# The radial matmuls of a graph network's second layer on two row groups of TensorE, with the bias as three bf16 parts put in first

## The chip, the cores and the metric

The kernel runs on one core of a Trainium2 chip, in one launch. The metric is the device time of that launch in microseconds. A smaller time is better.

## What is computed

The reference runs four graph layers over 12,500 nodes with 32 features each and 400,000 edges, sorted by destination. Each layer is followed by a sum with its own input and a layer norm. The change touches the second layer only. For it the reference is, cut to what matters:

```python
R = relu(abs_distances[:, None] @ w1 + b1) @ w2 + b2      # w1: 1x64, w2: 64xR_DIM (8x8 values for each path)
Y = spherical_harmonics(rel_vec)                          # Y[0], Y[1:4], Y[4:9] of each edge
Fj = features[src]                                        # 8 scalars and 8 vectors of 3
for i, (mo, lo) in enumerate(RS):                         # RS = [(8, 0), (8, 1)]
    for j, (mi, li) in enumerate(RS):
        Rb = R[:, r_off:r_off + sz].reshape(E, mo, mi, n_lf)
        for k, lf in enumerate(range(abs(lo - li), lo + li + 1)):
            acc = acc + _NORM[i] * einsum('euv,ef,evi,ofi->euo', Rb[..., k], Yf, Fb, C)
msg = concatenate(msg_blocks)                             # 32 values for each edge
out = zeros.at[dst].add(msg)
```

Each edge's distance goes through 64 hidden units into a row R of radial weights. In the kernel 384 of them (after scaling and sorting of the columns) multiply the edge's source features turned into its own frame. b2 is the bias of that row.

## The kernel before

The second layer goes over the edges in 196 groups of 2,048 edges: 128 partitions by T = 16 tiles, in four streams (ST = 4). One group is one `step`, and four groups make one turn of each engine's loop. The order of the work is written out by hand for each engine, and semaphores join them.

- **GpSimd (POOL), L1990 to L2005.** `gathers` issues 16 indirect DMAs for a group, one for each tile, that fetch the source rows into `xg`. There are two `xg` buffers. It waits for one to be free (`fxg`, L1996) and halfway for `half` (L2000), which TensorE raises when it comes to `radial` number 3.
- **SyncE (SP).** `load` brings the distances of a group into `wrow` (64 partitions, all 2,048 edges in each, so that each hidden unit has them), the source indices `s_i` and the nine frame numbers of each edge `e9`. `load_row` brings the flags for the segment sums.
- **ScalarE (ACT).** `hidden` makes `H` = relu(w1 x distance + b1) in partitions 0 to 63, for 2,048 edges in one instruction. Partitions 64 to 127 of `H` hold ones. `spread` copies the turned features into `FG` and `FX` with five copies and frees `xg`. `early_sums` copies the sums of the first four tiles out of PSUM. `scalars` and `scan_store` follow.
- **TensorE (PE).** For each group there are eight calls of `radial(n, u)`. Each makes the rows R of two tiles of 128 edges, tiles 2u and 2u+1, into the two banks of `pR[u % 2]`: one matmul over all 128 rows for each tile, f32, 384 columns. Row 64 of `w2` is the bias and rows 65 to 127 are zeros, so the ones in `H` add the bias. Between the calls stand the early sums (sixteen matmuls on the identity for tiles of u = 0 and 1), `turn` (three matmuls), `columns` and `back` (transposes). The order is radial 0, 1, back, radial 2, 3, early sums (first half), radial 4, early sums (second half), columns, radial 5, turn 0, radial 6, turn 1 and 2, radial 7.
- **VectorE (DVE).** `products(k, u)` waits for `pR` (L2066) and multiplies the two tiles' R with the features: for u = 0 and 1 in three instructions into `PP` (L2069, L2072), for the others in two into `Pr` (L2078, L2080). `sums(k, u)` waits for those products, raises `fpR` (the semaphore that lets TensorE write that `pR` again, L2259 in `radial`) and reduces over the 16 columns (L2089). `head` (L2058), three parts of `tail` and the segment `scan` stand in between.

The matmuls are recorded twice each for f32, since an f32 matmul is two passes over the array; the trace counts each pass. So one `radial` is four matmul records and four weight loads, and 196 groups by 8 by 4 give its 6,272 records.

## Time and profile before

| what | value |
|---|---|
| median of 3 runs | 18,546.1 us |
| lowest and highest run | 18,534.44 and 18,557.52 us |
| span of the profiled execution | 20,972.7 us |
| second layer's loop in that span | from about 6,660 to 12,480 us |

The profiled execution has no time of its own beside its span, and the span is longer than the median of the runs. All rows come from the profiled execution. A row of a timeline gives the start, the duration, the engine, the line, the operation, out<-in with the tile names, how many instructions were merged, and in brackets the idle time of that engine just before, with what ended it. A q behind the engine's name is its sequencer. PEclk is the share of TensorE's full clock that was granted: 1.00 is 2.4 GHz and 0.50 is 1.2 GHz.

### The profile page before, as it was taken

How to read it: one execution, taken by the hardware profiler on the slowest of the kernel's cores; microseconds unless marked ns; L12 is line 12 of the kernel's file. 1: busy time of each engine (PE TensorE's matmuls, PEld its weight loads, DVE VectorE, ACT ScalarE, POOL GpSimd, SP SyncE). 2: the span in 40 equal slices, each digit the busy share in tenths (PEclk: the TensorE clock that was granted, in tenths of full speed). 3: DMA queues.
4: the chain of work that ended last, by engine and by line, in shares of the span. 5: the costliest groups of instructions: out<-in, count | busy, mean ns of one | idle time of the engine just before them, and what ended most of it. 6: DMA issues, size and time to landing. Idle time of an engine off the chain costs nothing. (4 is left out here: it accounts for less than half of the span.)

```text
span 20972.7 us, 293199 instructions
## 1 busy us (share of the span) xinstructions
PE 13068.2 (62%) x92471; PEld 7362.5 (35%) x92471; DVE 11202.5 (53%) x19689; ACT 3071.4 (15%) x5120; POOL 11778.5 (56%) x10055
## 2 busy tenths in 40 slices
PE   0565555555554676776766652555555555699999
PEld 0344434333333444444444431122222112355554
DVE  2565544444444777777777773333332222567777
ACT  0222222222221111111111110111111111000000
POOL 4788888888886555555555554666666665100000
PEclk6565555555556888888888885666666666799999
DMA  7333333333333222222222213333333343489998
GB/s 276 47 39 37 37 39 39 39 37 37 38 39 46 47 49 47 48 47 47 48 46 48 46 40 35 73 70 72 76 71 71 71 76 63 125 257 293 292 293 267
DMA packets 2998639, 1817.14 MB, mean 87 GB/s; under 512 B 1730466, under 2 KB 2755819, under 8 KB 2979019
## 3 DMA queue, kind: packets, MB, share of 16 engines
q1 hardware_dynamic: 2201756, 1336.87, 25.1%
q0 software_dynamic: 669312, 166.80, 11.3%
q10 hardware_dynamic: 126512, 300.38, 4.1%
q8 instruction: 539, 8.83, 0.2%
q14 instruction: 520, 4.25, 0.1%
HBM read 1474.43 MB, written 392.90 MB: 89 GB/s over the span
## 5 line engine op out<-in xcount | busy, mean ns | idle before, releaser
L2005 POOL DMA_INDIRECT xg<-d_tab,s_i x3136 | 3254.6, 1038 | 2615.5 <-POOLq L1996 1630.7
L2537 POOL DMA_INDIRECT xg<-d_tab,s_i x3136 | 2996.6, 956 | 1865.8 <-issue 954.8
L2265 PE MATMUL pR<-w,H 128*128 128x384 f32 x6272 | 2703.4, 560 | 1407.6 <-PEq L2259 834.5
L1403 POOL DMA_INDIRECT d_acc<-AG,ix x1568 | 2471.5, 1576 | 527.2 <-issue 459.5
L1403 POOL DMA_INDIRECT d_acc<-T,ix x1568 | 2466.3, 1573 | 478.3 <-issue 437.1
L2923 PE MATMUL pacc<-nodes,HB 128*32 128x512 fp8e4 x47040 | 2663.0, 380 | 42.7 <-PEq L2967 42.7
L2574 DVE TENSOR_TENSOR_SCAN U<-mU,U,up 128x512 f32<-128x512 f32 x392 | 501.6, 1280 | 3289.0 <-DVEq L2573 2688.6
L2265 PEld LDWEIGHTS pR<-w,H 128*128 128x128 f32 x6272 | 1225.8, 215 | 2533.1 <-issue 2182.8
L2695 PE MATMUL hb<-U,Wbc 128*128 128x512 f32 x784 | 642.4, 914 | 2204.7 <-PEq L2691 2023.1
L1756 PE MATMUL pm<-ms,eq 128*128 128x32 f32 x6272 | 1366.4, 399 | 890.5 <-PEq L1754 888.8
L2923 PEld LDWEIGHTS pacc<-nodes,HB 128*32 128x32 f16 x47040 | 1261.5, 97 | 1317.1 <-issue 57.1
L1756 PEld LDWEIGHTS pm<-ms,eq 128*128 128x128 f32 x6272 | 1344.1, 330 | 934.8 <-issue 934.4
L1035 PE MATMUL pw<-ok,ol 128*128 128x392 bf16 x4048 | 1303.7, 458 | 319.3 <-PEq L1033 299.3
L1023 DVE TENSOR_SCALAR ok<-iotak,kt 128x392 bf16<-128x392 f16 x4048 | 1372.9, 390 | 0.0
L2892 DVE TENSOR_SCALAR nodes<-packed 128x1792 int32<-128x1792 int32 x840 | 918.0, 1093 | 756.3 <-DVEq L2890 755.3
L2078 DVE TENSOR_TENSOR AG<-pR,FG 128x512 f32<-128x512 f32 x784 | 538.0, 686 | 950.3 <-DVEq L2066 893.7
L2695 PEld LDWEIGHTS hb<-U,Wbc 128*128 128x128 f32 x784 | 191.4, 283 | 2313.3 <-issue 2308.3
L2089 DVE TENSOR_REDUCE Q<-AG 128x64 f32<-128x1024 f32 x784 | 948.3, 1210 | 0.0
L2893 DVE TENSOR_SCALAR nodes<-packed 128x1792 int32<-128x1792 int32 x840 | 912.4, 1086 | 0.0
L1718 PE MATMUL sr<-ids,two 2*128 2x512 bf16 x784 | 411.6, 525 | 798.2 <-PEq L1721 794.9
L2271 PE MATMUL pQ<-PP,ident 128*128 128x128 f32 x6272 | 806.4, 281 | 120.4 <-issue 117.9
L2271 PEld LDWEIGHTS pQ<-PP,ident 128*128 128x128 f32 x6272 | 795.8, 197 | 209.0 <-issue 109.7
(338 smaller groups left out, 17504.3 us busy)
## 6 DMA issues: line engine op xcount, KB each, us to landing
packed<-d_A SPq DMA_DIRECT2D x420, 1792.0 KB
row<-d_m SPq DMA_DIRECT2D x1568, 64.0 KB
xg<-d_tab,s_i POOLq DMA_INDIRECT x6272
wrow<-d_w SPq DMA_DIRECT2D x196, 512.0 KB
d_scan<-so ACTq DMA_DIRECT2D x392, 256.0 KB
d_A<-stage ACTq DMA_DIRECT2D x97, 784.0 KB
d_ea<-in_ea_t ACTq DMA_DIRECT2D x1, 50176.0 KB
d_exp<-T ACTq DMA_DIRECT2D x1, 50176.0 KB, 250.4
```

Source lines behind the costliest of these rows:

```text
L1023: last = e.tensor_scalar(ok[:, i, :], A["iotak"][:, :], kt[:, 2, s + i:s + i + 1], kt[:, 1, s + i:s + i + 1], ALU.is_equal, ALU.mult)
L1035: last = e.matmul(A["pw"][w % 2][:, 0:KW], A["ol"][u % RU][:, i, :], A["ok"][u % RU][:, i, :], start=(u % 2 == 0 and i == 0), stop=(u % 2 ...
L1403: e.indirect_dma_start(out=d_acc[i], out_offset=bass.IndirectOffsetOnAxis(ap=ix[k][:, t:t + 1], axis=0), in_=mo[k][:, t * F:(t + 1) * F], ...
L1756: last = e.matmul(pm[:, t, :], eq[k][:, t, :], ms[:, t % CH * ST + t // CH, :], start=True, stop=True)
L2005: e.indirect_dma_start(out=xg[k][:, t, :], out_offset=None, in_=d_tab, in_offset=bass.IndirectOffsetOnAxis(ap=s_i[n][:, t:t + 1], axis=0)) ...
L2089: e.tensor_reduce(Q[k][:, :, 2 * u:2 * u + 2, :].rearrange("p r t u -> p t r u"), Pr[u % 3].rearrange("p t (r u) c -> p t r u c", u=8), ax ...
L2265: last = e.matmul(pR[u % 2][:, j, 0:384], H[k][:, (2 * u + j) * P:(2 * u + j + 1) * P], w2[:, :], start=True, stop=True)
L2271: last = e.matmul(pQ[:, :, :], ident[:, :], PP[:, :, :, c, :].rearrange("p u t r -> p (u t) r"), start=(c == 0), stop=(c == 15))
L2537: e.indirect_dma_start(out=xg[n][:, j * ST + c, :], out_offset=None, in_=d_tab, in_offset=bass.IndirectOffsetOnAxis(ap=s_i[d][:, col:col + ...
L2892: e.tensor_scalar(low, both, SMALL, None, ALU.bitwise_and)
L2893: e.tensor_scalar(high, both, 4, SMALL, ALU.logical_shift_right, ALU.bitwise_and).then_inc(S(f"un{u}"), 1)
L2923: end = e.matmul(pacc[k][32 * g:32 * (g + 1), :], HB[i][:, b0 + bb, 32 * h:32 * (h + 1)], of, start=(begins and h == 0), stop=(ends and h ...
```

## The change

The radial matmuls use half of the array's rows each. `H` now has 1,024 columns: partitions 0 to 63 hold the hidden units of tiles 0 to 7, and partitions 64 to 127 those of tiles 8 to 15. `radial(n, u)` makes tiles u and u+8, one on rows 0 to 63 and the other on rows 64 to 127. The weights `w2` stand in both halves. The bias no longer has a row of `w2`. It is split into three bf16 parts, put into three rows of a bf16 tile `b2s` that is zero elsewhere (in each half), and a matmul of a tile of ones with it goes ahead of each radial matmul in the same PSUM bank.

What follows from it: two DMAs of `wrow` for a group instead of one, `hidden` over 128 partitions by 1,024 elements, one more copy in `spread` (six) and in `early_sums` (two), other strides for `products` and `sums`, and a longer preparation ahead of the loop (12 loads of weights, six products and sums, three roundings with two subtractions, six one-row DMAs, and TensorE waits for those).

```diff
-            wrow = [sb(st, f"wrow{n}", [64, GE]) for n in range(DEEP)]
-            H = [sb(st, f"H{k}", [P, GE]) for k in range(2)]
+            wrow = [sb(st, f"wrow{n}", [P, GE // 2]) for n in range(DEEP)]
+            H = [sb(st, f"H{k}", [P, GE // 2]) for k in range(2)]
...
+            b2s = sb(st, "b2s", [P, 384], BF16)
+            onesr = sb(st, "onesr", [P, P], BF16)
...
-            FX = [sb(st, f"FX{k}", [P, T, 2, 16]) for k in range(2)]
+            FX = [sb(st, f"FX{k}", [P, T // 2, 2, 2, 16]) for k in range(2)]
...
-                        e.dma_start(wrow[n][:, :].rearrange("h (c n) -> h c n", c=ST), bc(w_v[:, bass.ds(s * SW, SW)], 0, 64)
-                                    ).then_inc(S(f"w{n}"), 16)
+                        for h in range(2):
+                            e.dma_start(wrow[n][64 * h:64 * h + 64, :].rearrange("h (c n) -> h c n", c=2),
+                                        bc(w_v[2 * h:2 * h + 2, bass.ds(s * SW, SW)], 0, 64)).then_inc(S(f"w{n}"), 16)
...
+                    load(0, 0, sources=False)
+                    load(0, 1, sources=False)
+                    e.wait_ge(S("bp"), 1)
+                    e.sem_inc(S("bp"), -1)
+                    for h in range(2):
+                        for i in range(3):
+                            row = 64 * h + i
+                            e.dma_start(b2s[row:row + 1, :], b2p[i][row:row + 1, :]).then_inc(S("lb"), 16)
+                    load(0, 2, sources=False)
...
+                    for i in range(3):
+                        e.tensor_copy(b2p[i][:, :], b2t[0][:, :]).then_inc(S("vc"), 1)
...
+                        if i < 2:
+                            e.tensor_tensor(b2t[0][:, :], b2t[0][:, :], b2p[i][:, :], ALU.subtract).then_inc(S("vc"), 1)
...
-                        j, t = u % 2, slice(2 * u, 2 * u + 2)
+                        j, t = u % 2, slice(u, T, 8)
...
-                        e.tensor_reduce(Q[k][:, :, 2 * u:2 * u + 2, :].rearrange("p r t u -> p t r u"),
+                        e.tensor_reduce(Q[k][:, :, u:T:8, :].rearrange("p r t u -> p t r u"),
...
-                        e.activation(H[k][0:64, :], wrow[n][:, :], ACT.Relu, bias=b1c[:, 0:1],
+                        e.activation(H[k][:, :], wrow[n][:, :], ACT.Relu, bias=b1c[:, 0:1],
...
-                        e.activation(FX[k][:, :, :, 0:8], turned[:, 1:3, :, :].rearrange("p o t v -> p t o v"), ACT.Copy
-                                     ).then_inc(S("ca"), 1)
+                        for h in range(2):
+                            e.activation(FX[k][:, :, h, :, 0:8],
+                                         turned[:, 1:3, 8 * h:8 * h + 8, :].rearrange("p o u v -> p u o v"), ACT.Copy
+                                         ).then_inc(S("ca"), 1)
...
-                        e.activation(Q[k][:, :, 0:4, :].rearrange("p r t u -> p t r u"),
-                                     pQ[:, :, :].rearrange("p t (r u) -> p t r u", u=8), ACT.Copy).then_inc(S("qc"), 1)
+                        for h in range(2):
+                            e.activation(Q[k][:, :, 8 * h:8 * h + 2, :].rearrange("p r t u -> p t r u"),
+                                         pQ[:, :, h, :].rearrange("p t (r u) -> p t r u", u=8), ACT.Copy
+                                         ).then_inc(S("qc"), 1)
...
+                    e.wait_ge(S("lb"), 96)
+                    e.sem_inc(S("lb"), -96)
...
                         for j in range(2):
-                            last = e.matmul(pR[u % 2][:, j, 0:384], H[k][:, (2 * u + j) * P:(2 * u + j + 1) * P], w2[:, :],
-                                            start=True, stop=True)
+                            half = slice(64 * j, 64 * j + 64)
+                            e.matmul(pR[u % 2][:, j, 0:384], onesr[half, :], b2s[half, :], start=True, stop=False)
+                        for j in range(2):
+                            half = slice(64 * j, 64 * j + 64)
+                            last = e.matmul(pR[u % 2][:, j, 0:384], H[k][half, u * P:(u + 1) * P], w2[half, :],
+                                            start=False, stop=True)
                         last.then_inc(S("pR"), 1)
```

## Rows read from the trace of the kernel before

**Rows 1.** The page: span, and busy time of each engine over the span.
```profile
span 20972.7 us, 293199 instructions
PE 13068.2 (62%) x92471; PEld 7362.5 (35%) x92471; DVE 11202.5 (53%) x19689; ACT 3071.4 (15%) x5120; POOL 11778.5 (56%) x10055
```

**Rows 2.** Second layer's loop in one window: engines' busy time, PEclk, DMA share, GB/s.
```profile
6660.00:12480.00 5820.00, 4051.08 (x15280) 2486.89 (x15278) 4280.10 (x6070) 830.91 (x1762) 3235.76 (x3117) 0.86 0.22 47
```

**Rows 3.** DVE waits in that window: us in total, times, longest us.
```profile
DVE AG L2078 <- DVEq L2066: 893.7, 265, 19.2
DVE T L2078 <- DVEq L2066: 303.9, 142, 9.4
```

**Rows 4.** Timeline of DVE in the last group, no gathers running.
```profile
12438.06 0.68 DVE L2069 TENSOR_TENSOR PP<-pR,FG 128x512 f32<-128x512 f32 x1
...
12449.05 0.70 DVE L2078 TENSOR_TENSOR T<-pR,FG 128x512 f32<-128x512 f32 x1
...
12459.57 0.70 DVE L2069 TENSOR_TENSOR PP<-pR,FG 128x512 f32<-128x512 f32 x1
```

**Rows 5.** Timeline of the same group: TensorE.
```profile
12439.70 1.53 PE L2265 MATMUL pR<-w,H 128*128 128x384 f32 x4 [0.86 <-PEq L2259]
...
12442.85 1.46 PE L2265 MATMUL pR<-w,H 128*128 128x384 f32 x4
...
12446.46 0.63 PE L2297 MATMUL tp<-ident,mg 128*128 128x128 f32 x4 [0.36 <-PEq L2295]
...
12446.92 1.46 PE L2265 MATMUL pR<-w,H 128*128 128x384 f32 x4
```

**Rows 6.** Radial matmuls of all groups: duration ns min/median/max.
```profile
L2265 PE MATMUL pR<-w,H x6272: 486/486/981, 6663.1 to 12473.5; 128*128 128x384 f32 x196
```

**Rows 7.** A stretch of five us in a group with gathers, columns as in rows 2.
```profile
9020.00:9025.00 5.00, 0.00 (x0) 0.00 (x0) 0.00 (x0) 0.00 (x0) 3.77 (x4) 0.50 0.16 29
```

**Rows 8.** Timeline around that stretch.
```profile
9025.22 0.94 POOL L2005 DMA_INDIRECT xg<-d_tab,s_i  x1 [0.30 <-issue]
9029.07 0.69 DVE L2078 TENSOR_TENSOR AG<-pR,FG 128x512 f32<-128x512 f32 x1 [11.60 <-DVEq L2066]
...
9029.41 2.90 PE L2265 MATMUL pR<-w,H 128*128 128x384 f32 x4 [11.58 <-PEq L2259]
...
9032.45 0.69 DVE L2078 TENSOR_TENSOR T<-pR,FG 128x512 f32<-128x512 f32 x1 [0.97 <-DVEq L2066]
...
9038.68 0.94 POOL L2005 DMA_INDIRECT xg<-d_tab,s_i  x1 [12.52 <-POOLq L1996]
```

**Rows 9.** Third layer, PE timeline: 128-row and 64-row matmuls in turn, full clock.
```profile
14007.31 1.02 PE L2695 MATMUL hb<-U,Wbc 128*128 128x512 f32 x2
14008.26 1.12 PE L2696 MATMUL hb<-XT,Wa 64*128 64x512 f32 x2
14009.31 0.65 PE L2666 MATMUL up<-ident,ef 128*128 128x128 f32 x4
```

**Rows 10.** The same two lines by form in that stretch: busy us, mean ns.
```profile
L2696 PE MATMUL hb<-XT,Wa 64*128 64x512 f32 x2 | 1.1, 641 | 0.0
L2695 PE MATMUL hb<-U,Wbc 128*128 128x512 f32 x2 | 1.0, 592 | 0.0
```

**Rows 11.** A bf16 matmul of 392 columns, PE timeline of the third layer, full clock.
```profile
14011.34 0.84 PE L1035 MATMUL pw<-ok,ol 128*128 128x392 bf16 x4
```

**Rows 12.** ACT in the last group: timeline.
```profile
12452.26 0.38 ACT L2190 ACTIVATE FX<-turned 128x256 f32<-128x256 f32 x1
12452.52 0.28 ACT L2192 ACTIVATE FX<-turned 128x128 f32<-128x128 f32 x1
12452.68 0.29 ACT L2193 ACTIVATE FX<-turned 128x128 f32<-128x128 f32 x1
```

**Rows 13.** Timeline ahead of the loop: weights ready, first matmul.
```profile
6637.10 0.55 DVE L2042 TENSOR_TENSOR w<-w,w2x 65x384 f32<-65x384 f32 x1
...
6659.12 4.18 PE L2281 MATMUL turned<-hp,ident 128*128 128x384 f32 x6 [46.13 <-DVE hp L2058]
```

More of the change, by code:

```diff
@@ L1906, in gnn_kernel @@
             w2 = sb(st, "w2", [P, 384])
-            w2x = sb(st, "w2x", [65, 384])
-            cm = sb(st, "cm", [65, 384])
-            cx = sb(st, "cx", [65, 384])
-            w1c = sb(st, "w1c", [64, 1])
-            b1c = sb(st, "b1c", [64, 1])
+            w2t = [sb(st, f"w2t{n}", [P, 384]) for n in range(3)]
+            b2t = [sb(st, f"b2t{n}", [P, 384]) for n in range(4)]
+            b2p = [sb(st, f"b2p{n}", [P, 384], BF16) for n in range(3)]
+            b2s = sb(st, "b2s", [P, 384], BF16)
+            onesr = sb(st, "onesr", [P, P], BF16)
+            w1c = sb(st, "w1c", [P, 1])
+            b1c = sb(st, "b1c", [P, 1])
             FG = [sb(st, f"FG{k}", [P, T, 16]) for k in range(2)]
-            FX = [sb(st, f"FX{k}", [P, T, 2, 16]) for k in range(2)]
+            FX = [sb(st, f"FX{k}", [P, T // 2, 2, 2, 16]) for k in range(2)]
             hp = sb(st, "hp", [P, 3, 3, T, 8])
@@ L1945, in _ @@
                         load_sources(0, n)
[L1946 to L1951 removed]
+                    for h in range(2):
+                        half = slice(64 * h, 64 * h + 64)
+                        e.dma_start(w1c[half, :], a["w1"].rearrange("a h -> h a")).then_inc(S("lw"), 16)
+                        e.dma_start(b1c[half, :], a["b1"].rearrange("(h a) -> h a", a=1)).then_inc(S("lw"), 16)
+                        for dst, name in ((w2, "w2m"), (w2t[0], "w2x"), (w2t[1], "cm"), (w2t[2], "cx")):
+                            e.dma_start(dst[half, :], a[name][0:64, :]).then_inc(S("ld"), 16)
+                    for dst, name in zip(b2t, ("w2m", "w2x", "cm", "cx")):
+                        e.dma_start(dst[:, :], a[name][64:65, :].broadcast_to([P, 384])).then_inc(S("ld"), 16)
                     def load(a_, n, sources=True):
@@ L1964, in load @@
                                     d_fr[bass.ds(s + 4, 1), :, :].rearrange("a p x -> (a p) x")).then_inc(S(f"le{n}"), 16)
-                    for n in range(3):
-                        load(0, n, sources=False)
+                    load(0, 0, sources=False)
[7 more added lines that the diff above has]
+                    load(0, 2, sources=False)
                     with e.Fori(0, G // 4 - 1) as it:
@@ L2025, in _ @@
                 def _(e):
-                    for k in range(2):
-                        e.memset(H[k][64:P, :], 1.0).then_inc(S("vc"), 1)
+                    e.memset(onesr[:, :], 1.0).then_inc(S("vz"), 1)
+                    e.memset(b2s[:, :], 0.0).then_inc(S("vz"), 1)
+                    e.wait_ge(S("ld"), 192)
+                    e.sem_inc(S("ld"), -192)
+                    e.tensor_tensor(b2t[0][:, :], b2t[0][:, :], b2t[2][:, :], ALU.mult).then_inc(S("vc"), 1)
+                    e.tensor_tensor(b2t[1][:, :], b2t[1][:, :], b2t[3][:, :], ALU.mult).then_inc(S("vc"), 1)
@@ new lines, in _ @@
+                    e.tensor_tensor(w2[:, :], w2[:, :], w2t[1][:, :], ALU.mult).then_inc(S("vc"), 1)
+                    e.tensor_tensor(w2t[0][:, :], w2t[0][:, :], w2t[2][:, :], ALU.mult).then_inc(S("vc"), 1)
+                    e.wait_ge(S("vc"), 4)
+                    e.sem_inc(S("vc"), -4)
+                    e.tensor_tensor(b2t[0][:, :], b2t[0][:, :], b2t[1][:, :], ALU.add).then_inc(S("vc"), 1)
+                    e.tensor_tensor(w2[:, :], w2[:, :], w2t[0][:, :], ALU.add).then_inc(S("vc"), 1)
@@ L2152, in _ @@
                     sums(1, 7)
-                    e.wait_ge(S("qc"), 1)
-                    e.sem_inc(S("qc"), -1)
+                    e.wait_ge(S("qc"), 2)
+                    e.sem_inc(S("qc"), -2)
                     for part in range(3):
@@ L2202, in early_sums @@
                         e.sem_inc(S("pQ"), -1)
-                        e.activation(Q[k][:, :, 0:4, :].rearrange("p r t u -> p t r u"),
-                                     pQ[:, :, :].rearrange("p t (r u) -> p t r u", u=8), ACT.Copy).then_inc(S("qc"), 1)
+                        for h in range(2):
+                            e.activation(Q[k][:, :, 8 * h:8 * h + 2, :].rearrange("p r t u -> p t r u"),
+                                         pQ[:, :, h, :].rearrange("p t (r u) -> p t r u", u=8), ACT.Copy
+                                         ).then_inc(S("qc"), 1)
                     def scalars(k):
@@ L2270, in early_sums @@
                         for c in range(c0, c1):
-                            last = e.matmul(pQ[:, :, :], ident[:, :],
+                            last = e.matmul(pQ[:, :, :, :].rearrange("p u t r -> p (u t) r"), ident[:, :],
                                             PP[:, :, :, c, :].rearrange("p u t r -> p (u t) r"), start=(c == 0), stop=(c == 15))
```

54 lines of the change are left out of this document (21 added, 33 removed).

## The prediction

> **What bounds the kernel now.** I read the page's head first [rows 1]: no engine is busy for more than 62% of the span, so the stage has to be read by itself. The window over the second layer's loop [rows 2] shows 5,820 us, or 29.69 us for each of 196 groups. VectorE is busy for 4,280 us of it (21.84 us a group), TensorE for 4,051 us and GpSimd for 3,236 us. DVE is the fullest, but it also stands idle for 5,820 - 4,280 = 1,540 us, 7.86 us a group.
>
> The list of DVE's waits [rows 3] puts 893.7 and 303.9 us of that on line L2066, the wait for `pR`. That looks like TensorE being late with the radial rows, so I went to the timelines. In the last group, when no gather runs any more [rows 4], DVE comes from one second product of a group to the next in 12,459.57 - 12,438.06 = 21.51 us, back to back. TensorE is then ahead: its radial 5 ends at 12,446.92 + 1.46 = 12,448.38 [rows 5], and the product that reads it starts at 12,449.05 [rows 4], 0.67 us later. So at full clock DVE sets the pace and TensorE has slack.
>
> The other kind of group is seen in [rows 7, 8]. For five microseconds PE, DVE and ACT do nothing at all while POOL issues gathers, with 0.50 of the clock granted. DVE stays idle 11.60 us and goes on at 9,029.07, 2.9 us after the last gather of that batch ended (9,025.22 + 0.94). PE goes on at the same time, so PE's lateness didn't cause this hold. But what follows it does depend on PE: the first radial call takes 2.90 us instead of 1.46 [rows 5, 8], and the next product waits 0.97 us. The next batch of gathers starts at 9,038.68, 9.6 us after the hold's end, and it waits for `xg`, which is freed behind radial 5, radial 6, `turn` and `spread`. A hold costs about 11.60 + 0.97 = 12.6 us, so at most 1,540 / 12.6 = 122 groups can have one.
>
> The profiled span is 20,972.7 us and the median of the runs 18,546.1, so 2,426.6 us (13%) of the span are in no ordinary run. The rows don't say how much of that are holds. A price that hangs on held groups is therefore at most what I compute from the trace, and may be near nothing. A price in unheld groups counts in full. I add the sum to 18,546.1, since the stage's own work is the same in both. 0.2% is 37 us, or 0.19 us a group; less can't be told from no change.
>
> **Matmuls.** Before, a radial call is four passes. From 1.46 us for four and 0.486 for the last [rows 5, 6] a pass takes (1.46 - 0.49) / 3 = 0.32 us at full clock, so a call is 1.28 us of array time, and 2.56 at half clock. After, the two tiles sit on different rows and can run together. The order of issue is bias 0, bias 1, then both passes of tile 0, then both of tile 1. If matmuls start in their order, tile 0's second pass runs beside tile 1's first, so three slots of 0.32 remain. A bias matmul is one bf16 pass of 384 columns: half an f32 pass, 0.16 us, and at most 0.84 / 4 = 0.21 [rows 11]. I take 0.16 and count the two biases as one slot. The call is then 0.16 + 0.96 = 1.12 us, 0.16 less than now; at half clock 0.32 less. No row shows two row groups at once, so the bounds are full overlap, 0.16 + 0.64 = 0.80 us (0.48 less), and none, 2 x 0.16 + 1.28 = 1.60 us (0.32 more). I take the middle because of the order of issue.
>
> The Trainium skill, page "TensorE: Matmul & The Clock Gate", Part 3, says that matmuls on different row groups run concurrently but start and end strictly in program order. By that rule the call has three slots, which is the value taken; no row here shows it.
>
> **Changing between 128 and 64 rows.** The other matmuls keep all 128 rows, and they stand between radial calls. The third layer has such a change there and back [rows 9, 10]. A 512-column pass is spaced 1.02 - 0.59 = 0.43 us. From the start of L2695 to that of L2666 there are four passes, 1.72 us, but it takes 14,009.31 - 14,007.31 = 2.00 us. The 0.28 over is 0.14 for each change; I take 0.15, and 0.3 at half clock. The lower end is nothing, where PE was idle anyway.
>
> The Trainium skill, page "TensorEngine Tiling (Array Packing)", Key Properties, says that changing the tiling mode drains the engine. This speaks against the change, and the 0.14 us above agrees with it. Without the drain the sum would lose its changes of rows; with it, it stays as written.
>
> **Unheld groups.** The tightest path runs from radial 3 to the end of radial 5: three calls and four changes of rows (before and after each half of the early sums, and behind `columns`). That is 3 x -0.16 + 4 x 0.15 = +0.12 us, under the 0.67 of slack, beside 0.36 us in which PE now waits ahead of `columns` [rows 5]. The cost is nothing: DVE covers it. If that cover went, it would cost 0.12 x 196 = 24 us.
>
> **Held groups.** From the hold's end to the next gathers there are radial 5 and 6 at half clock, -0.64 us, and three changes of rows, +0.9. ACT's `spread` is on this path too. Its 128x256 copy takes 12,452.52 - 12,452.26 = 0.26 us of ACT's time, and a 128x128 one 0.16 [rows 12], so two of those instead cost +0.06. The net is +0.32 us, at most 122 times: 39 us. The lower end is zero, with no holds. I take 15 us.
>
> **The rest.** DVE's instructions keep their number and element counts; only strides over tiles change. I cost that at nothing. If strides did cost, there is no cover at all on DVE, and 0.01 us on each of 31 instructions of a group would be 61 us. `hidden` goes from 2.08 us over 2,048 columns to 1,024 columns, and `early_sums` gets a copy of 0.16 us. ACT is busy for 831 of 5,820 us [rows 2], so both are hidden. The second `wrow` DMA moves half the bytes, so the bytes in total stay, and SP issues one more DMA. Behind it on SP wait `s_i`, `e9` and the row flags, which are loaded groups ahead; the DMA share is 0.22 [rows 2]. The preparation grows by a chain of rounding, six one-row DMAs and a wait on TensorE. Now the weights are ready at 6,637.65 and PE first needs them at 6,659.12 [rows 13], when the first features arrive. So 21 us hide it; I estimate the growth as under 10 us. Without that cover it would be those 10 us, once.
>
> The sum is 0 + 15 + 0 = +15 us: **18,561 us**, which can't be told from no change.
>
> **Rivals.**
> - *Full overlap (faster).* All passes of the two tiles pair up and a call is 0.80 us. In unheld groups DVE hides it as before. In held ones the path loses 2 x 0.96 and gains 0.96 (changes of rows and the copy), so 0.96 x 122 = 117 us: 18,429 us. If also the 0.97 us wait behind each hold is a separate loss, another 118 us go: 18,311. For it speaks the time booked on L2066 [rows 3]. Against it speaks that most of that is the holds themselves, in which PE is idle too [rows 7].
> - *A part of it (faster).* Three slots, but more of DVE's small waits at half clock go than changes of rows add. Some 40 to 100 us, around 18,480.
> - *The row groups don't overlap (slower).* The change then does not do what it says. A call is 0.32 us longer. The path to radial 5 grows by 0.96 + 0.60 = 1.56 us; less the slack of 0.67 and perhaps the 0.36, 0.53 to 0.89 us are left, times 196: 104 to 174 us. Held groups add 2 x 0.64 + 0.9 + 0.06 = 2.24 us, at most 273 in all. About 18,546 + 140 + 120 = 18,806 us. It decides once a call is over 0.1 us longer than now.
> - *The clock (slower).* PE is busy for less of the time and the granted clock falls in groups that now keep 1.00. The path from radial 3 to the end of radial 5 takes 8.68 us [rows 5] and would double; less the slack, 8.0 us for such a group. With one in ten groups, 160 us: 18,706. It decides from five groups. Against it: in this layer the clock fell when PE stood still [rows 7], not when it worked half the time.
> - *Changes of rows dearer than taken (slower).* At 0.3 us at full clock the path grows by 0.72 us, 0.05 over the slack, and held groups add up to 60 us: 18,620.
>
> **How the numbers follow.** No change within 0.2%: 0.38. Full overlap 0.20 and a part of it 0.14, so faster: 0.34. No overlap 0.11, the clock 0.08 and dear changes of rows 0.09, so slower: 0.28. The range goes down to the far end of full overlap, 18,320, and up to about the middle of the no-overlap case, 18,800. Nearly 2 in 10 lie outside: beyond the far ends, and in what the rows can't show of ordinary runs. The likeliest case's own range is 18,510 to 18,585.
>
> **What the changed kernel's profile would show.** The radial call: matmul starts of tile 0's second pass and tile 1's first together mean three slots; a call of about 1.3 us with its tail is right, 1.0 means full overlap, 1.8 none. A gap of 0.1 to 0.2 us where rows change. DVE at 21.5 us a group where nothing is held. DVE's durations unchanged on L2078 and L2089. PEclk still about 0.86 in the loop. The first matmul of the layer still right behind the first `hp`. What would make the prediction wrong: a different number of holds, since each is worth 12 us and I take it as unchanged with no cause known for them; five fewer or more in ordinary runs outweigh all terms above.

## The result and the profile after

The changed kernel takes 18,443.18 us (median of 4 runs, 18,435.87 to 18,459.31). The kernel before takes 18,546.96 in its runs beside it. The ratio is 0.9946 (95% interval 0.9934 to 0.9958), so the change saves about 104 us, 0.54%. I had forecast no change that can be told, at 18,561 us.

First a correction to the ground I stood on. The profiled execution of before was 13% longer than any timed run, and the long holds of [rows 7, 8] were in no other profile (DVE's longest wait in [rows 3] is 19.2 us, in the same stretch of every later profile at most 6.3). So before was run and profiled once more, unchanged (the first experiment), and from here on "before" means that profile. Its span is an ordinary one:

```profile
span 18558.8 us, 293199 instructions
```

The page of the changed kernel, its head and the rows of the radial matmuls, the gathers and the `wrow` loads:

```profile
span 18439.3 us, 300421 instructions
...
PE 12519.4 (68%) x95607; PEld 6807.1 (37%) x95607; DVE 11147.9 (60%) x19696; ACT 2930.3 (16%) x5512; POOL 11894.6 (65%) x10055
...
L2017 POOL DMA_INDIRECT xg<-d_tab,s_i x3136 | 3333.5, 1063 | 1122.4 <-issue 579.9
...
L2295 PE MATMUL pR<-w,H 64*128 64x384 f32 x6272 | 1539.4, 569 | 0.0
...
wrow<-d_w SPq DMA_DIRECT2D x392, 256.0 KB
```

The same stretch of the layer's loop in both, 4,200 us long, columns as in [rows 2]; first before:

```profile
6700.00:10900.00 4200.00, 3405.68 (x14282) 2139.47 (x14281) 3960.48 (x5676) 778.05 (x1648) 3079.74 (x2932) 0.97 0.28 61
```

and the changed kernel:

```profile
6700.00:10900.00 4200.00, 3262.05 (x17664) 1828.82 (x17664) 4053.54 (x5825) 660.63 (x2066) 3201.11 (x3006) 0.87 0.29 62
```

GpSimd's last count divided by 16 gathers gives the groups: 183.25 before and 187.88 after, so 22.92 and 22.36 us a group. The 0.56 us less, times 196, are about 110 us: the whole gain lies in this loop. DVE's work in a group has not changed (3,960.48 / 183.25 = 21.61, 4,053.54 / 187.88 = 21.58 us). Its idle time has: 1.31 us a group before and 0.78 after. That is what has to be explained.

Did the radial calls get shorter? TensorE's timeline in one group of the changed kernel, columns as in [rows 5]:

```profile
9003.10 0.50 PE L2292 MATMUL pR<-b2s,onesr 64*128 64x384 bf16 x2 [2.51 <-PEq L2285]
9003.37 1.51 PE L2295 MATMUL pR<-w,H 64*128 64x384 f32 x4
...
9011.34 0.34 PE L2292 MATMUL pR<-b2s,onesr 64*128 64x384 bf16 x2
9011.51 0.81 PE L2295 MATMUL pR<-w,H 64*128 64x384 f32 x4
9012.25 2.05 PE L2301 MATMUL pQ<-PP,ident 128*128 128x128 f32 x16
```

Yes, and by more than I took. Four f32 passes of 0.32 us end within 0.81 us, tail included, so they run two and two: 0.64 us. The two bias matmuls take 0.17 together. A call is 0.80 us of array time, my lower bound, not 1.12. From the bias (9,011.34) to the next 128-row matmul (9,012.25) are 0.91 us, so the change of rows behind a call costs 0.11 us; I took 0.15. At half clock (the two rows at 9,003, granted clock 0.50 from 9,003 to 9,005) the call is about twice as long. The rule of the Trainium skill that I weighed (page "TensorE: Matmul & The Clock Gate", Part 3: row groups run concurrently, but start in program order) gives three slots. The trace shows two, so the measurement decides against it. The same skill's drain at a change of tiling mode ("TensorEngine Tiling (Array Packing)", Key Properties) agrees with the 0.11 us.

So the mechanism that I gave to the rival of full overlap is there. Whether it is what pays is another question. DVE's waits in this stretch, before:

```profile
DVE hp L2058 <- DVEq L2055: 110.9, 78, 5.1
DVE PP L2069 <- DVEq L2066: 74.6, 49, 1.8
DVE PP L2072 <- issue: 31.8, 46, 1.1
DVE T L2078 <- DVEq L2066: 22.0, 40, 1.9
```

and after:

```profile
DVE hp L2076 <- DVEq L2073: 144.1, 124, 3.8
DVE T L2096 <- DVEq L2084: 1.2, 1, 1.2
```

The waits for `pR` (line 2066, now 2084) are gone but for one of 1.2 us; before they were 74.6 + 22.0 = 96.6 us. The wait of `head` for the gathers is now the only one of size. A second row of before stands out: 46 times, once in every turn of four groups, line 2072 stops for 0.7 us on "issue", that is on nothing that the profile can name.

### The profile page after: what moved, and what is told of

It is laid out like the page before. It is cut to its first block and busy times, and to the rows that moved or that the text cites. A ratio compares the mean times of both kernels' runs of the same rounds, so it can differ in the third digit from the quotient of the medians.

```text
span 18439.3 us, 300421 instructions
## 1 busy us (share of the span) xinstructions
PE 12519.4 (68%) x95607; PEld 6807.1 (37%) x95607; DVE 11147.9 (60%) x19696; ACT 2930.3 (16%) x5512; POOL 11894.6 (65%) x10055
## 3 DMA queue, kind: packets, MB, share of 16 engines
q14 instruction: 286, 2.34, 0.0%
## 5 line engine op out<-in xcount | busy, mean ns | idle before, releaser
L2017 POOL DMA_INDIRECT xg<-d_tab,s_i x3136 | 3333.5, 1063 | 1122.4 <-issue 579.9
L2567 POOL DMA_INDIRECT xg<-d_tab,s_i x3136 | 2994.4, 955 | 957.9 <-issue 903.0
L2295 PE MATMUL pR<-w,H 64*128 64x384 f32 x6272 | 1539.4, 569 | 0.0
L2292 PE MATMUL pR<-b2s,onesr 64*128 64x384 bf16 x3136 | 596.7, 371 | 912.9 <-PEq L2285 909.1
L2301 PE MATMUL pQ<-PP,ident 128*128 128x128 f32 x6272 | 873.4, 296 | 0.0
L2704 PE MATMUL xp<-ident,xg 128*128 128x128 f32 x784 | 197.7, 402 | 969.9 <-DMA xg<-d_tab,s_i 969.9
L1453 DVE TENSOR_SCALAR ix<-nf,dump 128x16 int32<-128x16 f32 x196 | 48.9, 249 | 1330.6 <-DVEq L1452 1330.6
L1035 PEld LDWEIGHTS pw<-ok,ol 128*128 128x128 bf16 x4048 | 441.0, 128 | 1079.9 <-issue 1025.7
```

What stands on the lines that cost most here:

```text
L1035: last = e.matmul(A["pw"][w % 2][:, 0:KW], A["ol"][u % RU][:, i, :], A["ok"][u % RU][:, i, :], start=(u % 2 == 0 and i == 0), stop=(u % 2 ...
L2017: e.indirect_dma_start(out=xg[k][:, t, :], out_offset=None, in_=d_tab, in_offset=bass.IndirectOffsetOnAxis(ap=s_i[n][:, t:t + 1], axis=0)) ...
L2295: last = e.matmul(pR[u % 2][:, j, 0:384], H[k][half, u * P:(u + 1) * P], w2[half, :], start=False, stop=True)
L2301: last = e.matmul(pQ[:, :, :, :].rearrange("p u t r -> p (u t) r"), ident[:, :], PP[:, :, :, c, :].rearrange("p u t r -> p (u t) r"), star ...
L2567: e.indirect_dma_start(out=xg[n][:, j * ST + c, :], out_offset=None, in_=d_tab, in_offset=bass.IndirectOffsetOnAxis(ap=s_i[d][:, col:col + ...
```

## The experiments

Each ratio is to the unchanged kernel run beside it on the same chip, with its 95% interval. They are told in the order of the questions; "groups" as above are counted from the 4,200 us window.

### Is it the short call?

**Before, unchanged**, for an ordinary profile.

> The kernel before, unchanged, for a second profile. If the holds of the first profile belong to that one execution, the span comes out near 18,545 us, the second layer's loop takes about 4,490 us (the changed kernel's 4,387 plus the 104 us that it gained), 22.9 us a group, and no stretch of 5 us has DVE, PE and ACT all idle. If the holds belong to the kernel, the span is again near 20,970 and the loop takes 5,820 us. The time itself is within 0.1% of before either way. Theory A (the gain is TensorE's): the 0.5 us a group that the changed kernel saved show as waits that hang on TensorE, either DVE on pR or GpSimd on xg, which is freed behind TensorE's turn. Theory B (the gain is ScalarE's or the loads'): they show behind the hidden units or the distances, and TensorE is ahead of everything.

Measured: 18,558.09 us, 0.9998 (0.9989 to 1.0008). The rows above are its own. No hold in it: DVE's longest wait in the loop is 5.1 us.

**Tiles issued in turn** in the changed kernel: bias and radial matmul of tile u, then both of tile u+8.

```diff
                             e.matmul(pR[u % 2][:, j, 0:384], onesr[half, :], b2s[half, :], start=True, stop=False)
-                        for j in range(2):
-                            half = slice(64 * j, 64 * j + 64)
                             last = e.matmul(pR[u % 2][:, j, 0:384], H[k][half, u * P:(u + 1) * P], w2[half, :],
```

> The changed kernel, but with tile 0's bias and radial matmul issued before tile 1's bias and radial matmul. In the changed kernel's trace a call runs its passes in pairs and takes 0.80 us of array time. With this order I expect tile 1's bias to start only beside tile 0's last pass or after it, so a call of 1.1 to 1.3 us. Theory A: a part of the gain goes, ratio to before 0.996 to 1.000. Theory B: ratio 0.9945 as the changed kernel.

Measured: 18,439.36 us, 0.9936 (0.992 to 0.9953). Its call looks the same:

```profile
9001.75 0.34 PE L2292 MATMUL pR<-b2s,onesr 64*128 64x384 bf16 x2
9001.91 0.83 PE L2293 MATMUL pR<-w,H 64*128 64x384 f32 x4
```

In both kernels the starts come in pairs, 3 to 25 ns apart. The records don't name the tile, but matmuls on the same 64 rows run one after the other (the next experiment: 1.45 us for four passes, not 0.83), so a pair is one pass of each tile. The second tile's matmuls then don't wait for the first's three passes that are issued ahead of them: program order doesn't hold between row groups here.

**Both tiles on the same 64 rows**, in the kernel before: the bias matmuls are added and the radial matmuls use rows 0 to 63 for both tiles, so the passes of the two tiles can't run beside each other. The rounding of the bias also puts instructions ahead of DVE's loop.

```diff
-                            last = e.matmul(pR[u % 2][:, j, 0:384], H[k][:, (2 * u + j) * P:(2 * u + j + 1) * P], w2[:, :],
-                                            start=True, stop=True)
+                            e.matmul(pR[u % 2][:, j, 0:384], onesr[0:64, :], b2s[0:64, :], start=True, stop=False)
+                        for j in range(2):
+                            last = e.matmul(pR[u % 2][:, j, 0:384], H[k][0:64, (2 * u + j) * P:(2 * u + j + 1) * P],
+                                            w2[0:64, :], start=False, stop=True)
```

> The kernel before with its hidden units in 64 partitions, one load and one ScalarE instruction for them, but with 64-row matmuls on rows 0 to 63 for both tiles and the bias as three bf16 parts ahead. Nothing can overlap: a call is 2 x 0.16 + 1.28 = 1.60 us, and TensorE changes between 64 and 128 rows as often as in the changed kernel. Theory A: slower than before by 0.3 to 1.5% (0.3 us on each of three calls and 0.6 us of row changes in a path with 0.7 us of slack, times 196, and more at half clock). Theory B: within 0.2% of before.

Measured: 18,698.82 us, 1.0073 (1.0056 to 1.009). A longer call does cost. DVE then waits for `pR`:

```profile
DVE T L2099 <- DVEq L2087: 180.4, 185, 1.9
DVE AG L2099 <- DVEq L2087: 99.5, 42, 2.9
```

**No bias matmuls** in the changed kernel: b2 is left out of the result.

```diff
-                            e.matmul(pR[u % 2][:, j, 0:384], onesr[half, :], b2s[half, :], start=True, stop=False)
-                        for j in range(2):
-                            half = slice(64 * j, 64 * j + 64)
...
-                                            start=False, stop=True)
+                                            start=True, stop=True)
```

> The changed kernel without the bias matmuls; it leaves the second layer's b2 out. A call falls from 0.80 to 0.64 us of array time. Theory A with TensorE still in the pacing path: 8 x 0.16 x 196 = 250 us at the very most, and if only the calls ahead of turn count, 20 to 60 us, ratio to before 0.991 to 0.994. If TensorE has left the path, the ratio stays 0.9945. Theory B: 0.9945.

Measured: 18,450.43 us, 0.9941 (0.9925 to 0.9958): no better than the changed kernel.

**The bias matmul four times** in the changed kernel (each starts the sum afresh, so only the last counts and the result is the same), which brings the call back to 4 x 0.16 + 0.64 = 1.28 us, what it was before.

```diff
-                            e.matmul(pR[u % 2][:, j, 0:384], onesr[half, :], b2s[half, :], start=True, stop=False)
+                            for r in range(4):
+                                e.matmul(pR[u % 2][:, j, 0:384], onesr[half, :], b2s[half, :], start=True, stop=(r < 3))
```

> The changed kernel with each bias matmul issued four times in place of once (the last one counts), so that a call is 4 x 0.16 + 0.64 = 1.28 us at full clock and 2.56 at half, just as before the change, with the row changes on top. Theory A: VectorE waits for pR again, ratio 0.999 to 1.004. Theory B: ratio stays 0.9945.

Measured: 18,434.85 us, 0.9943 (0.9927 to 0.996). The trace has the long call, 9,001.38 - 8,999.97 = 1.41 us with the change of rows behind it:

```profile
8999.97 0.83 PE L2293 MATMUL pR<-b2s,onesr 64*128 64x384 bf16 x8
9000.63 0.82 PE L2296 MATMUL pR<-w,H 64*128 64x384 f32 x4
9001.38 1.56 PE L2312 MATMUL turned<-hp,ident 128*128 128x384 f32 x4
```

That is the result that turned the study. With the old length of the call the whole gain is still there.

**`hidden` in two instructions** of 64 partitions by 1,024 columns, ACT's saving taken back.

```diff
-                        e.activation(H[k][:, :], wrow[n][:, :], ACT.Relu, bias=b1c[:, 0:1],
-                                     scale=w1c[:, 0:1]).then_inc(S(f"H{k}"), 1)
+                        for h in range(2):
+                            half = slice(64 * h, 64 * h + 64)
+                            e.activation(H[k][half, :], wrow[n][half, :], ACT.Relu, bias=b1c[half, 0:1],
+                                         scale=w1c[half, 0:1]).then_inc(S(f"H{k}"), 1)
```

> The changed kernel with the hidden units made by two ScalarE instructions of 64 partitions by 1,024 elements (about 1.2 us each) in place of one of 128 by 1,024, so that ScalarE is as long on them as before the change. Theory A (the calls on two row groups are short enough that VectorE no longer waits for them once in a loop turn): ratio to before 0.9945, as the changed kernel. Theory B (the shorter ScalarE instruction is what pays): the gain goes, ratio 0.999 to 1.000.

Measured: 18,437.93 us, 0.9946 (0.993 to 0.9963). ACT carries none of it.

**`H` and `w2` in bf16** in the kernel before (coarser rows R), a call of 0.32 us.

> The kernel before with H and w2 rounded to bf16, which changes the precision of the second layer's radial weights. A call is then two passes of 0.16 us, 0.32 us at full clock and 0.64 at half, on all 128 rows, with no row groups, no extra loads and no change of rows. Theory A: VectorE's waits for pR (0.6 us a group in the second profile of before) vanish, ratio 0.993 to 0.995, and what stays is the wait for the gathers. Theory B: 0.999 to 1.000.

Measured: 18,511.03 us, 0.9985 (0.9975 to 0.9994). A call far shorter than the changed kernel's gives about a quarter of its gain. (It keeps the stops on "issue" that the next section is about: 46 of them, 55.4 us.)

**Fifteen gathers a group** in the changed kernel; tile 15's features are a constant.

```diff
-                        for t in range(T):
+                        for t in range(T - 1):
```

> The changed kernel with 15 gathers a group in place of 16; the features of tile 15 are left out (a constant stands there). GpSimd's batch takes 22.35 us a group in the changed kernel's trace, just the loop's period, and VectorE waits 0.78 us a group for the gathers ahead of head. If GpSimd sets the pace of the changed kernel, the period falls to VectorE's own 21.5 to 21.6 us, 0.8 us a group or about 155 us, ratio 0.986 to 0.987. If VectorE's wait there is only swapped for another, ratio 0.992 to 0.9945.

Measured: 18,323.87 us, 0.9885 (0.9869 to 0.9902), 0.6% below the changed kernel. One gather in sixteen less on GpSimd and the loop is faster: it is GpSimd that sets the pace. The loop's group falls to 4,200 x 15 / 2,873 = 21.93 us, by 0.43 us and not by a whole gather's 1.25, for then DVE's own 21.66 us are nearly reached.

### The stop on "issue": where the code lies

The page lists the DMA queues; its last one fetches instructions (columns: packets, MB, share). Before:

```profile
q14 instruction: 519, 4.25, 0.1%
```

and changed:

```profile
q14 instruction: 286, 2.34, 0.0%
```

The 233 more, of 8 KB each, come five in each turn of DVE's loop: the first 1.0 us after DVE's jump back, two more within the next 6 us, the others some 45 and 84 us after the jump. Before, around such a turn:

```profile
8503.58 0.41 DVE L2072 TENSOR_TENSOR PP<-pR,FX 128x256 f32<-128x256 f32 x1
8504.77 0.95 POOL L2005 DMA_INDIRECT xg<-d_tab,s_i  x1 [2.51 <-issue]
8504.78 0.42 DVE L2072 TENSOR_TENSOR PP<-pR,FX 128x256 f32<-128x256 f32 x1 [0.79 <-issue]
...
8505.08 2.90 PE L2265 MATMUL pR<-w,H 128*128 128x384 f32 x4 [4.29 <-PEq L2259]
...
8508.13 0.69 DVE L2069 TENSOR_TENSOR PP<-pR,FG 128x512 f32<-128x512 f32 x1 [1.80 <-DVEq L2066]
```

DVE stops 0.79 us in the middle of its products. TensorE, which stood idle for 4.29 us, comes back at half clock, 0.50 in the window's row for the three microseconds behind it:

```profile
8505.00:8508.00 3.00, 2.92 (x6) 1.63 (x7) 1.33 (x2) 0.00 (x0) 2.39 (x3) 0.50 0.07 14
```

Its call takes 2.90 us and not 1.46, and DVE waits 1.80 us for it. The change adds nine instructions to DVE's queue ahead of the loop (five products, sums and subtractions, three roundings and two waits more, one memset fewer), so the loop's code lies nine instructions further on, and there are no such fetches.

**Nine small DVE instructions ahead of the loop** in the kernel before, nothing else.

```diff
+                    for c in range(8):
+                        e.memset(pad[:, c:c + 1], 0.0).then_inc(S("vp"), 1)
+                    e.wait_ge(S("vp"), 8)
+                    e.sem_inc(S("vp"), -8)
```

> The kernel before with nine small VectorE instructions (eight one-column memsets and their wait) ahead of the second layer's loop, while VectorE waits there for the first gathers anyway. The changed kernel has nine more VectorE instructions ahead of that loop than the kernel before (568 against 559 records). Theory C (the gain is where VectorE's loop lies in its instruction memory: before, the branch at each loop turn is followed by five fetches of 8 KB on queue 14 and VectorE stops; after, there are none): no fetches in the loop, ratio 0.994 to 0.995, with not one matmul changed. Theory A (the calls on two row groups): ratio 1.000. Both in part: in between.

Measured: 18,504.64 us, 0.9971 (0.996 to 0.9983). The queue's row and DVE's waits, `head`'s for the gathers and that for `pR` (now line 2071):

```profile
q14 instruction: 285, 2.33, 0.0%
```

```profile
DVE hp L2063 <- DVEq L2060: 195.2, 152, 5.0
DVE T L2083 <- DVEq L2071: 15.9, 20, 2.1
```

The fetches and the stop on "issue" are gone, and of 96.6 us of waits for `pR` 15.9 are left, with the old matmuls. Most of that is not gained: `head`'s wait for the gathers grows from 110.9 to 195.2 us in the same window.

**Four of them.**

> The kernel before with four such instructions, one look for the edge. Two more instructions (the kernel with bf16 calls) still fetched 232 blocks in 4,200 us of the loop, nine more did not. Theory C: either about 230 fetches and a time near before, or none and a time near 18,440 us, nothing between. Theory A: the time of before either way.

One run: 18,578.96 us beside 18,561.2 for before. 520 packets: the fetches stay. Four instructions are not enough.

**119 and 128 of them** in the changed kernel. With its own nine, 119 make 128 more than before.

> The changed kernel with 119 small VectorE instructions ahead of the loop, so that with its own nine it lies 128 instructions (8 KB at 64 bytes each, one fetch) behind the kernel before, in the same place within a block. Theory C, if only the place within a block counts: the fetches come back, five a loop turn, and the ratio goes to 0.998 to 1.000; what stays below 1 is what the row groups give at half clock. If the buffer's own edge counts and not the block's, the fetches may stay away: ratio 0.9945. Theory A: ratio 0.9945 with or without fetches.

> The changed kernel with 128 such instructions, one whole block, as the control for the padding itself. Theory C: the same place within a block as the changed kernel, no fetches in the loop, ratio 0.9945. If the padding costs time of its own (it takes some 10 us while VectorE waits for the first gathers), up to 0.9950.

Measured: 18,442.02 us, 0.9937 (0.9923 to 0.995), and 18,442.49 us, 0.9936 (0.992 to 0.9951). The fetches came back with 119 (521 packets) and not with 128 (288): the place counts, and a shift by 128 instructions leaves it as it was. But here the fetches cost nothing that can be told. The turn with 119:

```profile
8293.96 0.42 DVE L2095 TENSOR_TENSOR PP<-pR,FX 128x256 f32<-128x256 f32 x1 [0.61 <-issue]
8294.26 0.50 PE L2297 MATMUL pR<-b2s,onesr 64*128 64x384 bf16 x2 [5.17 <-PEq L2290]
...
8294.53 1.51 PE L2300 MATMUL pR<-w,H 64*128 64x384 f32 x4
...
8296.19 0.69 DVE L2092 TENSOR_TENSOR PP<-pR,FG 128x512 f32<-128x512 f32 x1 [0.68 <-DVEq L2089]
```

The stop and the half clock are the same, but the short call brings DVE's wait down from 1.80 to 0.68 us. So the row groups do cover a hole that the old call could not. In the changed kernel the hole isn't there.

The Trainium skill has the mechanism, which I had not weighed: page "Advanced Engine Details and Errata", section "ISA Cache", gives VectorE 32 KB for instructions in two lines of 256. My inference from it is that a loop that lies across one line more than fit has to be loaded anew in each turn. That agrees with fetches that come and go with the loop's place. The sizes don't: here a fetch is 4.25 - 2.34 = 1.91 MB / 233 = 8.2 KB, five come in each turn, and a shift by 128 instructions, half a line, is enough to bring the fetches back.

### The `wrow` load: large DMAs hold up the gathers

Nine instructions give 0.29% (0.17 to 0.40) of the 0.54%. The rest shows on GpSimd. SP's and GpSimd's timelines before, in one group:

```profile
8195.83 0.63 SPq L1957 DMA_DIRECT2D wrow<-d_w  x1
...
8202.08 0.95 POOL L2005 DMA_INDIRECT xg<-d_tab,s_i  x1 [1.58 <-DMA xg<-d_tab,s_i]
```

and changed:

```profile
8194.41 1.40 SPq L1962 DMA_DIRECT2D wrow<-d_w  x2
...
8199.92 0.94 POOL L2017 DMA_INDIRECT xg<-d_tab,s_i  x1 [0.56 <-issue]
8201.30 0.94 POOL L2017 DMA_INDIRECT xg<-d_tab,s_i  x1 [0.44 <-issue]
```

A gather follows its forerunner after 0.30 us when nothing is late. Some 6 us behind the 512 KB load one waits 1.58 us for an earlier gather's landing, 1.28 too long. Behind two loads of 256 KB the waits are 0.26 and 0.14 too long. The change cuts this load in two only because `wrow` now sits in two halves.

**Two loads, without and with the nine instructions**, in the kernel before, all matmuls as before.

```diff
-                        e.dma_start(wrow[n][:, :].rearrange("h (c n) -> h c n", c=ST), bc(w_v[:, bass.ds(s * SW, SW)], 0, 64)
-                                    ).then_inc(S(f"w{n}"), 16)
+                        for h in range(2):
+                            e.dma_start(wrow[n][:, GE // 2 * h:GE // 2 * (h + 1)].rearrange("h (c n) -> h c n", c=2),
+                                        bc(w_v[2 * h:2 * h + 2, bass.ds(s * SW, SW)], 0, 64)).then_inc(S(f"w{n}"), 16)
```

> The kernel before with the load of wrow in two DMAs and no padding, so that VectorE still fetches five blocks a loop turn. Theory D: the share of the load alone, ratio about 0.9965. If the fetches only cost time through the late half-clock calls on 128 rows, they keep costing it here. Theory A': 1.000.

> The kernel before with the nine instructions of padding (0.9971) and its 512 KB load of wrow split into two DMAs of two streams each, as the changed kernel has it; matmuls as before. In the padded kernel's trace GpSimd waits 618.5 us in 4,200 us of the loop for earlier gathers to land, with up to 2.1 us at a time; in the changed kernel's 425.7 us and 1.4. Theory D (the rest of the gain is the load in two pieces, which lets gathers land sooner): ratio 0.9935 to 0.9945 and about 425 us of that wait. Theory A' (the rest is the row groups'): ratio stays 0.997 with about 618 us of that wait.

Measured: 18,477.67 us, 0.9966 (0.9952 to 0.9979) for the loads alone, and 18,439.3 us, 0.9945 (0.9932 to 0.9959) for both. That is the changed kernel's time with neither row groups nor bias matmuls.

**Four loads** of 128 KB, in the changed kernel and in the kernel before with the nine instructions.

> The changed kernel with the load of wrow in four DMAs of 128 KB in place of two of 256 KB. Theory D, if the size of the piece is what counts: GpSimd's wait for landings falls further and the ratio goes to 0.992 to 0.993. If only the first split counts, or SP's issue time takes over: 0.9935 to 0.9945. Theory A': 0.9943.

> The kernel before with nine more small VectorE instructions ahead of the loop and the wrow load in four DMAs of 128 KB. If the loads alone carry the rest and the row groups give nothing, this is 0.990 of before (as the changed kernel with four loads, 0.9903). If the row groups give something once the gathers no longer land late, this stays above 0.992, between the changed kernel's 0.9946 and its four-load version.

Measured: 18,356.48 us, 0.9903 (0.9888 to 0.9918), and 18,370.1 us, 0.9904 (0.9888 to 0.9921). Again the row groups add nothing, and both beat both kernels of the study. GpSimd's waits (us in total, times, longest): all of them before, then those for landings with two loads and with four, both with the nine instructions:

```profile
POOL xg L2005 <- DMA xg<-d_tab,s_i: 607.9, 1352, 2.2
POOL xg L2005 <- issue: 497.5, 1551, 4.2
POOL xg L2005 <- POOLq L1996: 9.0, 18, 2.3
POOL xg L2005 <- POOLq L2000: 6.0, 11, 1.2
```

```profile
POOL xg L2007 <- DMA xg<-d_tab,s_i: 453.2, 1349, 1.5
```

```profile
POOL xg L2007 <- DMA xg<-d_tab,s_i: 454.3, 1490, 0.3
```

The 0.30 us that every wait for a landing has anyway is 405.6, 404.7 and 447.0 us of these; 202, 49 and 7 us are left over.

**Eight loads** of 64 KB in the changed kernel.

> The changed kernel with the wrow load in eight DMAs of 64 KB. With four the longest wait for a gather's landing is already 0.3 us, so the theory that large loads delay the gathers gives no more than 0.1% here: 0.990 +- 0.001. If it goes by the number of DMAs and not by how long a gather can be held up, another step of 0.3 to 0.4% follows: 0.986.

Measured: 18,353.19 us, 0.9897 (0.9881 to 0.9914). With four loads and the nine instructions no gather waited over 0.3 us for a landing, and eight loads find nothing left to gain.

**Two loads cut the other way**, by hidden units (32 partitions each) and not by streams, with the nine instructions.

> As the kernel with nine more VectorE instructions and two loads of wrow (0.9945), but the load is cut by hidden units (32 partitions each, all four streams) and not by streams. If the size of one DMA decides, it is 0.9945 again and the longest wait for a gather 1.4 to 1.5 us. If it was the cut by streams that helped, it stays at the single load's 0.997 with 2.1 us.

Measured: 18,458.11 us, 0.9953 (0.9937 to 0.997). The longest wait for a landing is 2.0 us, what is left over 0.30 us each is 539.2 - 1,387 x 0.30 = 123 us, between one load (215 in the run with nine instructions) and two by streams (49). The time can't tell it from either. So the size of one DMA isn't all; how the cut lies counts too, and why stays open.

The Trainium skill, page "DMA: Bandwidth & Descriptors", section "Queues, rings and completion order", says that a DMA engine changes from one queue to the next only when a whole packet is done. That a smaller load holds a gather up for less (2.2, 1.5, 0.3 us) agrees with it; that the cut by hidden units leaves 2.0 us at the same size is not explained by it, and what an engine drains at a time can't be read from these traces: the load's records are of 2,048 bytes in every variant.

### The groups side by side

From the same window of each: us a group, DVE's idle time in it, GpSimd's busy time (the gathers themselves), and GpSimd's idle time less 16 x 0.30 us. The last two and 4.8 us add up to the group.

| kernel | ratio | a group | DVE idle | gathers | GpSimd held up |
|---|---|---|---|---|---|
| before | 1 | 22.92 | 1.31 | 16.81 | 1.31 |
| nine instructions | 0.9971 | 22.73 | 1.14 | 16.59 | 1.34 |
| two loads | 0.9966 | 22.63 | 1.03 | 17.20 | 0.64 |
| nine instructions, two loads | 0.9945 | 22.41 | 0.84 | 17.04 | 0.57 |
| the changed kernel | 0.9946 | 22.36 | 0.78 | 17.04 | 0.52 |
| nine instructions, four loads | 0.9904 | 22.05 | 0.51 | 17.04 | 0.21 |
| changed, four loads | 0.9903 | 22.00 | 0.46 | 17.00 | 0.20 |
| no overlap (same rows) | 1.0073 | 23.69 | 1.95 | 16.80 | 2.09 |

DVE's own work stays at 21.55 to 21.61 us in all but the last (21.74). What moves is how long it stands idle. In the last row it is TensorE that is late, and GpSimd is held up by buffers that come free later (229.7 us of its waits there, 9.0 before).

The gathers' own length moves too. The nine instructions leave the holding up as it was (1.31 and 1.34 us) and win their 0.2 us in the gathers (16.81 to 16.59); the two loads take 0.67 us off the holding up and lose 0.39 of it to longer gathers. Most gathers take 0.94 us, some 1.1 to 3.1, and these fall together with certain DVE instructions: with the nine instructions, gathers of over 1.0 us fill 20% of the window, but 60% of the time of `head` lies under them, and only 2% of that of the product of `AG` and `FX`. So DVE and GpSimd are tied to each other by more than the semaphores. No run tests what makes a gather long, so by which way the stop in DVE's loop costs its 0.29% is not shown; that it goes with the fetches is.

## Why the prediction was wrong

**What failed** is the step that I called the rest. Of the second `wrow` DMA it says that the bytes stay and SP only issues one more, of the preparation that 21 us hide it, and it costs both at nothing. The load in two is worth 18,477.67 - 18,538.69 = -61 us alone (to the unchanged kernel beside it), and 0.9945 - 0.9971 = -0.26%, -48 us, on top of the nine instructions. The nine instructions that the preparation puts ahead of DVE's loop are worth 18,504.64 - 18,561.2 = -57 us alone, and 18,439.3 - 18,477.67 = -38 us on top of the two loads. Both together are -0.55%, and the changed kernel has -0.54%.

**What bounds the kernel.** I took DVE as the pace of unheld groups, 21.51 us [rows 4]. But [rows 4] is the last group, in which no gathers run, and I never measured an unheld group in the midst of the loop. Such a group takes 22.92 us, and DVE stands idle for 1.31 of it. So 1.4 us a group, 276 us in all, were open to any edit that helps what DVE waits for, and GpSimd is what sets the rest: of its 1,120 us without a gather in the window only 9.0 + 6.0 are waits for a free `xg` or for `half`, the others are the spacing of the gathers and waits for its own landings, and one gather less gives 0.6%. I saw GpSimd's 3,236 us in [rows 2] and read it as the third engine. The 0.30 us ahead of each gather, idle in that row, belong to its time too.

**Holds.** I put +15 us on held groups with at most 122 of them. In an ordinary run there is none, so the term is 0. The prediction warned that holds may be near nothing in the runs that are timed; that DVE's other waits need not be those of this profile either, it did not say.

**The call.** Taken as 1.12 us with 0.80 and 1.60 as bounds; measured 0.80. **Changes of rows**: taken as 0.15 us, measured 0.11. Both terms are in unheld groups, and I said that DVE hides them. That was right: a call of 0.64, 0.80 or 1.28 us gives 0.9941, 0.9946 and 0.9943, and the old matmuls the same with either number of loads. **No overlap**, the rival at 1.60 us: I worked out 104 to 174 us for unheld groups. Measured against the run with nine instructions (it too has no fetches, 285 packets), it is 18,698.82 - 18,504.64 = 194 us (189 by the ratios), somewhat above, and it came as a wait for `pR`, as I said.

**The rival of full overlap** names the right call and, by luck, nearly the right time (18,429 us): its price needs holds, of which there are none. **A part of it** (18,480 us) rests on DVE's small waits at half clock. Those waits were there, but the nine instructions alone take away all but 15.9 us of 96.6, with the old matmuls. **The clock**: its premise holds. The granted clock in the window falls from 0.97 to 0.87, but its price doesn't come: at half clock the call is 1.6 us, and DVE's list of waits has a single one on line 2084, of 1.2 us. With the bias four times the granted clock is 0.99 and the time the same.

**The signs that I named.** "1.0 means full overlap" is what the trace shows (0.17 + 0.81). The gap where rows change, 0.11 us, the durations on DVE's product and sum lines (within 0.01 us) and the first matmul behind `hp` stand as said. "DVE at 21.5 us a group" holds for its work (21.58 us) but not for the group, which takes 22.36 with nothing held. PEclk is 0.87, near the 0.86 that I named, but by luck: my 0.86 came from the profile with holds, and an ordinary one of before has 0.97.

## What to carry to other kernels

Before an engine is taken as the bound, compare its time in a group with the group's time in ordinary runs, in the midst of the loop and not in its last turn; the idle time that is left is what small edits to DMAs and queues can win. An edit has side effects that its diff doesn't call by name: a load cut in two, a loop's code nine instructions further on. When a gain comes, put those alone into the old kernel before the named part gets the credit. Here a load of 512 KB beside a stream of gathers is better issued as four of 128 KB.

## What the runs showed of the hardware that I had not expected

- Two row groups of 64 fully overlap, for f32 passes too, and, as the paired starts show, the second group's matmuls don't wait for the first's that stand ahead of them in the queue: four passes of 0.32 us within 0.81 us, issued either way.
- The place of a loop's code costs: five fetches of 8 KB for each turn of DVE's loop, a stop of 0.7 us on average before (31.8 us in 46 turns), 0.29% of the kernel. Nine instructions ahead of the loop took them away, four did not, and 128 more than before brought them back, though with the short calls they then cost nothing that can be told.
- With the load as one DMA of 512 KB the longest wait for a gather's landing was 2.2 us, with two of 256 KB 1.4 or 1.5 us (1.8 and 2.0 in the two runs that have the code fetches too, 2.2 with fifteen gathers a group, and 2.0 when cut the other way), with four of 128 KB 0.3 us, which is the spacing that gathers have anyway. What in the DMA engines holds them up wasn't measured.
- A gather's own time isn't fixed: most take 0.94 us, some up to 3.1, and the mean over the loop is 1.04 to 1.08 us from variant to variant. The cause was not tested.
